# Routed expert tiles on Trainium2: weights as the stationary operand of the gate and up products

## The reference, cut to what matters

```
def _mlp(x, gw, uw, dw):
    return jax.nn.silu(x @ gw.T) * (x @ uw.T) @ dw.T
...
top_v, top_i = jax.lax.top_k(scores, TOP_K)
mult = jax.nn.softmax(top_v, axis=-1)
...
for e in range(E):
    out = out + cw[:, e:e + 1] * _mlp(xf, gate_w[e], up_w[e], down_w[e])
...
return moe + shared
```

## Time and profile before

| | us |
|---|---|
| median of 3 runs | 3188.93 |
| the profiled execution | 3189.17 |
| its span | 3187.4 |
| routed tiles on TensorE | 2226.27 to 2560.1 of the span |
| TensorE busy over the span | 2873.4 |
| VectorE busy | 1317.2 |
| ScalarE busy | 835.8 |
| GpSimd busy | 812.0 |

### The profile page before, as it was taken

One profiled execution on the slowest core, in us unless ns is written; L12 is line 12 of the kernel. 1 busy time (PEld: TensorE's weight loads), 2 busy tenths in 40 slices (PEclk: granted clock), 3 DMA queues, 4 the chain that ended last, 5 costly groups with the idle time before them and its releaser, 6 DMA issues. The chain is left out here.

```text
span 3187.4 us, 70858 instructions
## 1 busy us (share of the span) xinstructions
PE 2873.4 (90%) x29244; PEld 1571.0 (49%) x29245; DVE 1317.2 (41%) x2655; ACT 835.8 (26%) x2170; POOL 812.0 (25%) x759
## 2 busy tenths in 40 slices
PE   6999999899999999999999999999999974009898
PEld 4666666534444444444444444387666643007555
DVE  5666666512332323333332323264222256986311
ACT  3554545411111111111111111131222256372111
POOL 2111111002222222222222222234444431004243
PEclk9999999999999999999999999999999987559899
DMA  6101010310000000000000000051222263005143
GB/s 212 58 26 32 26 32 26 120 36 17 24 16 18 24 16 21 20 18 23 18 18 23 18 23 18 17 210 44 44 45 45 44 182 90 0 1 210 51 119 73
DMA packets 78390, 164.11 MB, mean 51 GB/s; under 512 B 11787, under 2 KB 51567, under 8 KB 73110
## 3 DMA queue, kind: packets, MB, share of 16 engines
q1 hardware_dynamic: 53588, 104.04, 10.4%
q0 software_dynamic: 21456, 40.57, 5.7%
q10 hardware_dynamic: 3074, 15.45, 1.3%
HBM read 119.63 MB, written 40.37 MB: 50 GB/s over the span
## 5 line engine op out<-in xcount | busy, mean ns | idle before, releaser
L1072 PE MATMUL gru_ps_rz<-whh,scratch 128*32 128x512 f32 x6400 | 709.1, 595 | 0.0
L867 POOL TENSOR_TENSOR scratch<-scratch 128x1024 f32<-128x1024 f32 (+3 forms) x246 | 369.6, 1528 | 818.8 <-DVE stat L881 655.8
L1072 PEld LDWEIGHTS gru_ps_rz<-whh,scratch 128*32 128x32 f32 x6400 | 198.0, 110 | 453.5 <-issue 453.5
L1077 PE MATMUL gru_ps_n<-whh,scratch 128*32 128x256 f32 x6400 | 363.6, 379 | 0.0
L1001 DVE TENSOR_TENSOR scratch<-scratch,state 128x256 f32<-128x256 f32 x100 | 52.9, 529 | 666.7 <-ACT scratch L1030 666.7
L1077 PEld LDWEIGHTS gru_ps_n<-whh,scratch 128*32 128x32 f32 x6400 | 207.9, 110 | 180.1 <-issue 59.8
L472 DVE TENSOR_REDUCE att_neg_max<-att_banks 100x2 f32<-100x722 f32 x256 | 221.1, 906 | 134.0 <-PE att_banks L699 134.0
L1030 ACT ACTIVATE scratch<-gru_ps_rz 128x512 f32<-128x512 f32 x100 | 59.7, 597 | 726.0 <-PE gru_ps_rz L1072 726.0
L389 ACT ACTIVATE att_probsT<-att_banks 121x600 f32<-121x600 f32 x256 | 161.6, 670 | 183.7 <-PE att_banks L741 183.7
L1049 PE MATMUL gru_ps_rz<-wih,scratch 128*32 128x512 f32 x1600 | 191.4, 596 | 1.9 <-POOL scratch L969 1.9
L2388 PE MATMUL e_ps_g<-align_reach,ident 32*121 32x101 f32 x64 | 10.9, 326 | 197.1 <-DVE align_reach L2194 195.6
(11 more groups left out here) (400 smaller groups left out, 4160.9 us busy)
## 6 DMA issues: line engine op xcount, KB each, us to landing
table<-in_w SPq DMA_DIRECT2D x16, 1024.0 KB, 6.9
states<-state SPq DMA_DIRECT2D x100, 128.0 KB
scratch<-states SPq DMA_DIRECT2D x25, 512.0 KB, 3.6
whh<-in_whhT POOLq DMA_DIRECT2D x8, 1536.0 KB, 19.8
att_c_in<-in_ctxT SPq DMA_DIRECT2D x32, 363.0 KB, 3.0
dist_ctx<-in_ctxT SPq DMA_DIRECT2D x32, 363.0 KB, 4.4
align_ctx<-in_ctx_rows SPq DMA_DIRECT2D x32, 363.0 KB
whh<-in_guT ACTq DMA_DIRECT2D x8, 1024.0 KB, 11.9
```

The costliest lines, as they stand in the source:

```text
L867: done = nc.gpsimd.tensor_tensor(last.prod[:, row:row + rows, :], a, b, ALU.mult)
L1072: last = nc.tensor.matmul(ps_rz[quarter(q), :], stateT[c % 2][:, quarter(c // 2)], rz_columns(whh, c, q), start=False, stop=(c == GC - 1))
L1077: last = nc.tensor.matmul(ps_n[quarter(q), 0:GQ], stateT[c % 2][:, quarter(c // 2)], n_columns(whh, c, q), start=(c == 0), stop=(c == GC - 1))
```

## The change

Gate and up now have the expert's weights as the stationary operand: for each block of 128 hidden columns (FC = 4) and each half of the width (KT = 2) one matmul, whose weights are 128 by 128 of the expert's and whose moving operand is `xT`, 128 tokens wide. The result has the hidden columns on the partitions and the tokens along them, so `mid` is already as the down product needs it: the 4 transposes, `ps_m`'s use for them and the copy into `midT` go. For each tile VectorE copies the expert's 2048 columns of gate and up weights out of `experts_w` into one of two fixed places (`own_w`, in `scratch`), two tiles ahead, for which it loads the expert's number into a register itself (`fetch`).

```
+        own_w = [scratch[:, GU * u:GU * (u + 1)].rearrange("p (k h f) -> p k h f", k=KT, h=2) for u in range(2)]
...
-            def take_mid(n):
-                dve.wait_ge(m_turned, n + 1)
-                v.tensor_copy(midT.rearrange("p k n -> p (k n)"), ps_m[:, :]).then_inc(midT_ready, 1)
...
+            def fetch(n, u):
+                e = v.value_load(tile_expert[0:1, bass.ds(n, 1)], min_val=0, max_val=EXPERTS - 1)
+                v.tensor_copy(own_w[u].rearrange("p k h f -> p (k h f)"),
+                              experts_w[:, bass.ds(e, 1), 0:GU].rearrange("p a n -> p (a n)")).then_inc(own_w_ready, 1)
+
+            dve.wait_ge(tiles_ready, 1)
+            dve.wait_ge(experts_in, 16 * 2 * EXPERTS)
+            fetch(0, 0)
+            fetch(1, 1)
             product(0, 0)
-            take_mid(0)
+            fetch(2, 0)
             product(1, 1)
...
-            def up(psum, half, e, u):
-                for k in range(KT):
-                    done = nc.tensor.matmul(psum[:, :], xT[u][:, k, :],
-                                            experts_w[:, bass.ds(e, 1), k * 2 * FF + half * FF:k * 2 * FF + (half + 1) * FF].rearrange("p a n -> p (a n)"),
-                                            start=(k == 0), stop=(k == KT - 1))
+            def up(psum, half, u):
+                for c in range(FC):
+                    for k in range(KT):
+                        done = nc.tensor.matmul(psum[:, c * P:(c + 1) * P], own_w[u][:, k, half, c * P:(c + 1) * P], xT[u][:, k, :],
+                                                start=(k == 0), stop=(k == KT - 1))
                 return done
-            def turn_mid(n, u):
+            def down(n, u, e):
                 pe.wait_ge(mid_ready, n + 1)
                 for c in range(FC):
-                    done = nc.tensor.transpose(ps_m[:, c * P:(c + 1) * P], mid[u][:, c * P:(c + 1) * P], ident[:, :])
-                done.then_inc(m_turned, 1)
...
-                    done = nc.tensor.matmul(ps_y[:, 0:DIM], midT[:, c, :],
+                    done = nc.tensor.matmul(ps_y[:, 0:DIM], mid[u][:, c * P:(c + 1) * P],
...
-            def turn_of(n, u, here, before=None, after=None):
+            def turn_of(n, u, last_tile=False):
                 pe.wait_ge(xT_ready, n + 1)
-                if before is not None:
+                pe.wait_ge(own_w_ready, n + 1)
+                first = isinstance(n, int) and n == 0
+                if not first:
                     pe.wait_ge(act_ready, n)
-                up(ps_g[u], 0, here, u).then_inc(g_done, 1)
...
+                up(ps_g[u], 0, u).then_inc(g_done, 1)
+                up(ps_u[u], 1, u).then_inc(u_done, 1)
+                before = None if first else expert_of(n - 1)
+                if not last_tile:
                     turn_x(n + 1, 1 - u, 8 * (n + 1 - (1 - u)) + 16)
```

More of the change, by code:

```diff
@@ L1178, in mixture_stage @@
         mid = [room[:, 2 * FF + FF * u:2 * FF + FF * (u + 1)] for u in range(2)]
-        midT = room[:, 4 * FF:5 * FF].rearrange("p (k n) -> p k n", k=FC)
+        own_w = [scratch[:, GU * u:GU * (u + 1)].rearrange("p (k h f) -> p k h f", k=KT, h=2) for u in range(2)]
         y = [room[:, 5 * FF + DIM * u:5 * FF + DIM * (u + 1)] for u in range(2)]
@@ L1207, in mixture_stage @@
         g_done, u_done, act_ready, mid_ready = sem("g_done"), sem("u_done"), sem("act_ready"), sem("mid_ready")
-        m_turned, midT_ready, y_done, y_ready = sem("m_turned"), sem("midT_ready"), sem("y_done"), sem("y_ready")
+        y_done, y_ready, own_w_ready = sem("y_done"), sem("y_ready"), sem("own_w_ready")
         added = sem("added")
@@ L1623, in product @@
                 v.tensor_tensor(mid[u], act_g[u], ps_u[u][:, :], ALU.mult).then_inc(mid_ready, 1)
+            def fetch(n, u):
[6 more added lines that the diff above has]
+            fetch(1, 1)
             product(0, 0)
-            take_mid(0)
+            fetch(2, 0)
             product(1, 1)
-            take_mid(1)
+            fetch(3, 1)
             product(2, 0)
-            with dve.Fori(2, N // 2 + 1) as i:
-                take_mid(2 * i - 2)
+            fetch(4, 0)
+            with dve.Fori(2, N // 2) as i:
                 product(2 * i - 1, 1)
-                take_mid(2 * i - 1)
+                fetch(2 * i + 1, 1)
                 product(2 * i, 0)
-            take_mid(N - 1)
+                fetch(2 * i + 2, 0)
+            product(N - 2, 1)
+            product(N - 1, 0)
         @block.tensor
@@ L1695, in turn_x @@
                 done.then_inc(x_turned, 1)
-            def up(psum, half, e, u):
-                for k in range(KT):
-                    done = nc.tensor.matmul(psum[:, :], xT[u][:, k, :],
-                                            experts_w[:, bass.ds(e, 1), k * 2 * FF + half * FF:k * 2 * FF + (half + 1) * FF].rearrange("p a n -> p (a n)"),
-                                            start=(k == 0), stop=(k == KT - 1))
+            def up(psum, half, u):
[3 more added lines that the diff above has]
+                                                start=(k == 0), stop=(k == KT - 1))
                 return done
-            def turn_mid(n, u):
+            def down(n, u, e):
                 pe.wait_ge(mid_ready, n + 1)
                 for c in range(FC):
-                    done = nc.tensor.transpose(ps_m[:, c * P:(c + 1) * P], mid[u][:, c * P:(c + 1) * P], ident[:, :])
-                done.then_inc(m_turned, 1)
-            def down(n, e):
-                pe.wait_ge(midT_ready, n + 1)
-                for c in range(FC):
-                    done = nc.tensor.matmul(ps_y[:, 0:DIM], midT[:, c, :],
+                    done = nc.tensor.matmul(ps_y[:, 0:DIM], mid[u][:, c * P:(c + 1) * P],
                                             experts_w[:, bass.ds(e, 1), GU + c * DIM:GU + (c + 1) * DIM].rearrange("p a n -> p (a n)"),
@@ L1716, in down @@
                 done.then_inc(y_done, 1)
-            def turn_of(n, u, here, before=None, after=None):
+            def turn_of(n, u, last_tile=False):
                 pe.wait_ge(xT_ready, n + 1)
-                if before is not None:
+                pe.wait_ge(own_w_ready, n + 1)
+                first = isinstance(n, int) and n == 0
+                if not first:
                     pe.wait_ge(act_ready, n)
-                up(ps_g[u], 0, here, u).then_inc(g_done, 1)
[L1723 to L1728, removed]
+                up(ps_g[u], 0, u).then_inc(g_done, 1)
+                up(ps_u[u], 1, u).then_inc(u_done, 1)
+                before = None if first else expert_of(n - 1)
+                if not last_tile:
                     turn_x(n + 1, 1 - u, 8 * (n + 1 - (1 - u)) + 16)
-                if before is not None:
+                if not first:
                     if not isinstance(n, int) or n > 1:
                         pe.wait_ge(y_ready, n - 1)
[L1733 to L1739, removed]
+                    down(n - 1, 1 - u, before)
             pe.wait_ge(sy_ready, TT)
@@ L1744, in _ @@
             turn_x(0, 0, 16)
-            turn_of(0, 0, expert_of(0), after=False)
-            two_tiles(1)
+            turn_of(0, 0)
+            turn_of(1, 1)
+            turn_of(2, 0)
             with pe.Fori(2, N // 2) as i:
[L1748 to L1752, removed]
+                turn_of(2 * i - 1, 1)
+                turn_of(2 * i, 0)
+            turn_of(N - 2, 1)
+            turn_of(N - 1, 0, True)
             pe.wait_ge(y_ready, N - 1)
-            down(N - 1, after)
+            down(N - 1, 0, expert_of(N - 1))
 BANDS = 4
```

## The result

The changed kernel takes 3175.02 us (median of 6 runs, 3170.51 to 3177.84) against 3190.63 (6 runs, 3187.64 to 3194.83) for the kernel before: 15.6 us less, a ratio of 0.995 (95% interval 0.9939 to 0.9961). Measured once more on another occasion, 3176.97 against 3192.02, the ratio was 0.9946 (0.9932 to 0.996). The forecast was 3171.7, 17.5 us less than the profiled execution of before, with a range of 3164 to 3180.

The account below looks back on a forecast made before the run. The prediction took TensorE to bound the routed stretch: -24.6 us for transposes and +7.1 for shorter records, all else 0, took the profiled 3189.17 us down 17.5 to 3171.7, with a range of 3164 to 3180.

Parts of the forecast that it names:

- The bound: Routed tiles: TensorE, busy 332.17 of 334 us, bounds the stretch; the other engines are idle for more than half.
- Transposes, -24.6: TensorE, routed tiles: four transposes of mid per tile go, 0.44 us each set, 56 sets, 24.6 us saved.
- Records of 128 columns, +7.1: Gate and up on TensorE: 32 records per tile at 111.4 ns, 0.125 us more per tile, 7.1 us over 57.
- The lower, 107.5: Low end for gate and up: 107.5 ns per record, a 512-column record cut in four, nothing added.
- The upper, 118: High end for gate and up: 118 ns per record, from a run of 16 records, 19 us added in all.
- The copies, 0: VectorE, each tile: the added 2048-column weight copy, taken as 1.2 us, fits in slack and costs nothing.
- The bound of 2.29: VectorE's weight copy at one column per cycle: 2.29 us, the slow limit for one copy.
- GpSimd, 0: VectorE's copy and GpSimd's gather and add exclude each other in each tile, yet it costs nothing on either order.
- The forecast's timetable: Within a tile, a copy waiting for GpSimd's gather runs 2387.67 to 2388.9, clear of the add at 2389.09.
- The register load, 0: Loading the expert's number behind up, about 0.5 us of TensorE's sequencer, is covered by queued records and costs nothing.
- The ends, 0: Start and end of the routed stretch: first copy adds 0 to 0.2 us, taken as 0; the tail gains nothing itself.
- The sum: Whole kernel: -24.6 + 7.1 = -17.5 us, from 3189.17 to 3171.7.

Follow-up runs that it names:

- e3: The kernel before, with each 512-column stream of gate and up cut into 4 matmuls of 128, tokens still as weights; ratio 1.0017 to before, stretch 343.5 us.
- e5: The changed kernel with weight copies for the first two tiles only, later tiles reusing those weights; ratio 0.9945 to before, stretch 318.6 us.

## Why the prediction was right

- **The bound.** TensorE without a gap, the others with slack: it held, before and after, and in mid-stretch of every kernel here, down to a period of 5.38, but for the one with four copies per tile.
- **Transposes, -24.6.** Measured twice, 24.4 by putting them back and 24.5 by taking them out of the kernel before.
- **Records of 128 columns, +7.1.** Measured 8.0 (e3), and 7.8 is what the change's 16.6 leaves beside 24.4. The shared expert's rows give 0.89 / 8 = 111.3 ns, the forecast took 111.4 without saying why, and 111.6 was measured, in a run of 32. 57 times the 0.13 by which gate and up grew are 7.4; of the rest, 0.2 is the last add, below. Neither end of the range was reached. The lower, 107.5, was no bound: even a shorter load gives 109. The upper, 118, was read from 16 records that begin from an idle TensorE, and is no pace either: the first gate of the changed kernel begins so too and takes 1.89 for its 16 (2231.70 to 2233.59, 118 ns), the later ones 1.78. It is 0.1 us once.
- **The copies, 0.** Right, and with much more room than the sum said: three per tile would have cost nothing. 1.2 us was taken for one, from the way L1903 ended behind GpSimd; it is 1.23 alone, 1.45 where a gather holds it. The bound of 2.29 was not near.
- **GpSimd, 0.** The blocking came at the gather, and the adds were left alone (1.59 us as before). The forecast's timetable had only the copy wait for the gather; in every second tile of mid-stretch the gather waits for the copy instead and takes 1.80. It cost nothing on either order, as forecast, since the add comes later: after the long gather above, which ends at 2385.82, the next add is due at 2386.43.
- **The register load, 0.** Right on TensorE. On VectorE it was counted as 0.5 in the turn. In the changed kernel 0.15 to 0.28 us of it show between product and copy in most tiles; with four copies none of it does, which made that expectation wrong.
- **The ends, 0.** The first gate still waits for ScalarE, not for the copied weights. At the end the last add follows the one before by 4.44 us (2546.08 to 2550.52; 4.25 before), with its data ready at 2549.1: the tail is the adds' own, and 0.2 us longer than forecast.
- **The sum.** -17.5 forecast, -16.6 in the stretch, -15.6 between the medians, whose last us is within what the runs scatter. The mechanism was right term by term, and the miss of 0.9 lies mostly in the record's price and the last add.

The Trainium skill ("TensorE: Matmul & The Clock Gate", LDWEIGHTS) gives a load as its columns at 1.2 GHz, which for 128 columns is an estimate of 107 ns. Here the records with loads of 128 columns are 111.6 ns apart, whether 128 or 96 columns stream: the load is the limit, but some 5 ns dearer than the estimate. The sum by it, -24.6, was 8 us too good.

The Trainium skill ("SBUF — State Buffer", section "A bandwidth-pool intuition that's wrong (but worth ruling out)") has GpSimd's DMA blocked until about 115 ns after VectorE is done. The held gather above agrees: it ends at 2385.82, 0.11 us behind the copy's end at 2385.71. Which of the two is held isn't settled by which starts first, though: the gather starts first in every tile of mid-stretch, and in every second one the copy, 0.46 us behind it, goes ahead.

No kernel beside these is proposed: a record with the shorter load and one with the full load are within 3 ns of each other, so only fewer records would help, and dropping the copies, as e5 shows, would bring nothing.

## What to carry to other kernels

When an engine bounds a stretch without gaps, the sum of its own instructions is the forecast, and the starts of consecutive instructions, not their durations, give the price. A product's layout can be chosen so that the next product needs no turning; look for the price in the pieces the stream is cut into, and in the load that each piece carries. Work added to an idle engine is free up to its turn, but count what it holds up on another engine (here GpSimd's gather), and put it at a place of the period where that engine has nothing urgent.

## What the runs showed of the hardware

- A copy of 2048 float32 columns from SBUF to SBUF on VectorE takes 1.23 us, 0.60 ns per column, and it and GpSimd's indirect DMA instructions hold each other up. Who waits is decided by a tenth of a microsecond, and the two orders alternate through mid-stretch: a copy that follows 0.57 to 0.59 us after the gather's start (2379.09 against 2378.50) is held for 0.22 and takes 1.45; one that follows after 0.45 or 0.46 us (2384.48 against 2384.02) goes first, and the gather takes 1.80 in place of 0.99. The two copies that follow after 0.83 and 0.88 us aren't held, nor are their gathers.
- The engine's register load from SBUF (0.3 us) is done ahead by the sequencer while the engine works: it shows as no idle time on TensorE in mid-stretch, and as none on VectorE once it is full.
- Float32 matmuls of 128 columns with a load of 128 columns each are paced by the load, 111.6 ns from record to record; with 96 columns streamed it is the same, and with 96 columns loaded it is 109.
- Sixteen such records that begin from an idle TensorE take 0.1 us more than sixteen in mid-stretch (1.89 against 1.78), at the same granted clock of 1.00.
